# One hybrid network kernel: a ring of PSUM tiles in the first projections, router steps respaced in the dilated attention, second weights and results laid out anew

## The reference

```python
x = x + conv(groupnorm(x)); x = x + spiking_conv(groupnorm(x))   # x [16, 128, 28, 28]
t = tokens(x)                                # [16, 784, 128]
t = t + attention_8_heads(layernorm(t))      # softmax over 784 keys
t = t + top1_of_8_gelu_experts(layernorm(t))
t = t + dilated_attention_16_heads(layernorm(t))   # 256 tokens at rate 1, 512 at rate 2, 16 at rate 4
# last layer: two of 16 experts for each token, xn = layernorm(t)
top_vals, top_idx = top_k(xn @ gate_weight.T, 2); routing_w = softmax(top_vals)
h_mean[e] = sum over the tokens of e of silu(xn @ w1[e].T) / max(count[e], 1)
y_mean[e] = h_mean[e] @ w2[e].T              # [16, 128], zero where count is 0
t = t + sum over the two picks of routing_w * y_mean[top_idx]
```

## Time and profile before

| | |
|---|---|
| time before, median of 3 runs | 3283.76 us (3273.75 to 3286.78) |
| the profiled execution's own time | 3271.72 us |
| its span | 3270.0 us |
| TensorE / VectorE / ScalarE / GpSimd busy | 2786.8 / 2116.2 / 1555.8 / 1036.6 us |
| first projections | 179 to 351 us |
| dilated projections | 1845 to 2056 us |
| dilated attention | 2056 to 2876 us |
| second experts, to the last accumulation | 2903 to 3176 us |
| sums, means, second product | 3176 to 3222 us |
| results | 3222 to 3270 us |

### The profile page before, as it was taken

One profiled execution on the slowest core, in us unless ns is written; L12 is line 12 of the kernel. 1 busy time (PEld: TensorE's weight loads), 2 busy tenths in 40 slices (PEclk: granted clock), 3 DMA queues, 4 the chain that ended last, 5 costly groups with the idle time before them and its releaser, 6 DMA issues. The chain is left out here.

```text
span 3270.0 us, 64262 instructions
## 1 busy us (share of the span) xinstructions
PE 2786.8 (85%) x21148; PEld 1535.5 (47%) x21149; DVE 2116.2 (65%) x3960; ACT 1555.8 (48%) x3276; POOL 1036.6 (32%) x1355
## 2 busy tenths in 40 slices
PE   8978699999999999999399699588888788749998
PEld 4545134433333344333399577355555555413345
DVE  6745677777777777873322266677777777557762
ACT  2235266666666666667155333444544444324440
POOL 0023111222222322222333586245655655620000
PEclk9989699999999999999799899798898888769995
DMA  2024622223222322220322234333333322031132
GB/s 85 1 99 178 135 37 45 42 43 59 42 42 49 51 49 42 43 44 6 99 61 60 65 122 136 98 57 58 61 62 60 62 59 59 24 118 52 53 85 98
DMA packets 208762, 215.87 MB, mean 66 GB/s; under 512 B 32832, under 2 KB 184704, under 8 KB 208512
## 3 DMA queue, kind: packets, MB, share of 16 engines
q1 hardware_dynamic: 180768, 175.54, 23.4%
q0 software_dynamic: 14336, 25.72, 2.9%
q10 hardware_dynamic: 13424, 11.47, 1.2%
HBM read 129.29 MB, written 81.90 MB: 65 GB/s over the span
## 5 line engine op out<-in xcount | busy, mean ns | idle before, releaser
L1586 ACT ACTIVATE attn_exps<-attn_sbank 128x392 f32<-128x392 f32 x1600 | 704.7, 503 | 461.9 <-PE attn_sbank L1503 457.1
L1631 DVE TENSOR_REDUCE attn_mx<-attn_rot 128x1 f32<-128x784 f32 x768 | 722.0, 967 | 185.3 <-PE attn_rot L1516 182.4
L2360 ACT ACTIVATE dil_exps<-dil_sbank 128x512 f32<-128x512 f32 x512 | 289.2, 597 | 360.6 <-PE dil_sbank L2258 357.0
L1516 PE MATMUL attn_rot<-attn_k,attn_q 96*128 96x392 bf16 x1536 | 401.2, 344 | 67.9 <-DVE attn_mx L1631 39.4
L1503 PE MATMUL attn_sbank<-attn_q,attn_k 99*128 99x392 bf16 x1536 | 449.7, 333 | 10.9 <-ACT attn_exps L1586 9.7
L2416 DVE TENSOR_REDUCE dil_mx<-dil_rot 128x4 f32<-128x1024 f32 x256 | 307.3, 1218 | 70.2 <-PE dil_rot L2268 68.0
L1543 PE MATMUL attn_acc<-attn_exps,attn_v 128*32 128x392 f32 x3584 | 348.3, 500 | 0.0
L1503 PEld LDWEIGHTS attn_sbank<-attn_q,attn_k 99*128 99x128 bf16 x1536 | 148.6, 98 | 268.5 <-ACT attn_exps L1586 134.8
L2734 PE MATMUL silu_ph<-silu_route_w,silu_xT 128*128 x424 | 237.6, 645 | 16.7 <-issue 11.9
L1516 PEld LDWEIGHTS attn_rot<-attn_k,attn_q 96*128 96x128 bf16 x1536 | 117.2, 98 | 274.4 <-DVE attn_mx L1631 178.7
L2268 PE MATMUL dil_rot<-dil_k,dil_q 96*128 96x256 bf16 x1024 | 174.1, 299 | 79.7 <-DVE dil_mx L2416 49.1
(11 more groups left out here) (379 smaller groups left out, 4680.2 us busy)
## 6 DMA issues: line engine op xcount, KB each, us to landing
attn_q<-q_pieces SPq DMA_DIRECT2D x192, 98.0 KB, 3.4
attn_k<-k_pieces SPq DMA_DIRECT2D x192, 98.0 KB, 4.6
silu_x<-silu_rows SPq DMA_DIRECT2D x212, 64.0 KB
dil_q<-dil_q_pieces SPq DMA_DIRECT2D x192, 66.0 KB
dil_k<-dil_k_pieces SPq DMA_DIRECT2D x192, 66.0 KB
q_pieces<-qkv_piece SPq DMA_DIRECT2D x16, 588.0 KB, 3.1
k_pieces<-qkv_piece SPq DMA_DIRECT2D x16, 588.0 KB, 3.2
v_rows<-qkv_v SPq DMA_DIRECT2D x16, 476.0 KB, 3.8
```

Of the source, the lines that this page charges most:

```text
L1516: ins = nc.tensor.matmul(rot[b][:, hf, 0:HS], q[nxt.side][g][0:QROWS, j, c * P:(c + 1) * P], k_[nxt.side][g][0:QROWS, j, cols], start=True ...
L1586: nc.scalar.activation(e_[:, n % NP, :], sbank[(n + t.side) % 3][:, 0:HS], ACT.Exp, scale=A_DIM ** -0.5).then_inc(s_ex, 1)
L1631: nc.vector.tensor_reduce(into, rot[b][:, :, 0:HS], AX.XY, ALU.max).then_inc(s_free, 1)
L2360: nc.scalar.activation(e_[:, k % NP, :], sbank[k % 3][:], ACT.Exp, scale=D_DIM ** -0.5).then_inc(s_ex, 1)
```

## The change

It changes three places. The dilated projections, the 8-head attention and the first experts stay as they are.

**The ring, in `attn_inputs`.** The 16 images are written out, without a loop. Four PSUM tiles `pt` are taken in turns by five products of an image: centre and variance, rows, q, k, v. The weights of q, k and v are centred once (`wc`, three matmuls at the start), so that `xn` is `R` times the spread root and `xc` is gone; ScalarE squares the centred tile straight from PSUM. The rows are spread by four matmuls over 64 partitions each. Weights come from ACT's queue, the norm's constants from SP.

**The other end, in `experts_silu` and `finish`.** w2 has SBUF of its own and is loaded in 32 transfers of 128 KB during the tiles. The sums are 16 matmuls of 512 columns with 32 columns of weights, four experts side by side in the array; four copies, two on VectorE and two on ScalarE; 16 matmuls that turn the sums; one scaling into `mean` (in which only every 33rd column is other than zero; it is set to zero at the start); 64 products in four column groups; one product that adds the groups and leaves `ymean` on all 128 partitions. The gates lie at partitions 0, 32, 64 and 96, four images side by side, loaded by four transfers; in `finish` the products of four images use four row groups of the array.

**Dilated attention.** The steps of a turn are placed as in the diff; `rot`'s one semaphore becomes one for each tile; row copies and gate copies go from VectorE to ScalarE; `weigh` is cut into halves of four scores.

```diff
 # attn_inputs: PE's order for an image
+                def rows(n):
                     pe.wait_ge(s_rin, n + 1)
...
+                    for r in (0, 2, 1, 3):
+                        row = slice(64 * (r // 2), 64 * (r // 2) + 64)
+                        at = BANK * (r // 2) + BLK * (r % 2)
+                        ins = nc.tensor.matmul(rows_tile(n)[:, at:at + BLK], spread[row, r, :], rin[row, :], start=True, stop=True)
...
+                    pe.wait_ge(s_xn, n + 1)
+                    if n > 0:
+                        pe.wait_ge(s_rk, n)
+                    product(wc[:, 0, :], xn[j], q_tile(n)).then_inc(s_q, 1)
+                    if n + 1 < B:
+                        variance(n + 1)
+                    if n > 0:
+                        pe.wait_ge(s_vl, n)
+                    product(wc[:, 1, :], xn[j], k_tile(n)).then_inc(s_k, 1)
...
+                    if n + 1 < B:
+                        rows(n + 1)
+                    if n + 2 < B:
+                        pe.wait_ge(s_rq, n + 1)
+                        centre(n + 2)
...
+                    nc.scalar.activation(sq[:], centred_tile(n)[:, 0:S], ACT.Square).then_inc(s_sq, 1)
...
+                    nc.vector.tensor_tensor(halves(xn[n % 2][:]), halves(R[:, n, :]), banks(rows_tile(n)), ALU.mult).then_inc(s_xn, 1)
 # Router: copies on ScalarE
+    def act_rows(self, act, im, rot):
...
+        nc.scalar.activation(self.xc[:, 0:4, :], rot[0:TOK, 0, :].rearrange("k (c d) -> k c d", c=4), ACT.Copy)
...
-            ins = self.nc.vector.tensor_copy(self.turned[:, 4 * TOK * b:4 * TOK * b + cs * TOK], rot[0:self.ex.n, b, 0:cs * TOK])
+            ins = self.nc.scalar.activation(self.turned[:, 4 * TOK * b:4 * TOK * b + cs * TOK], rot[0:self.ex.n, b, 0:cs * TOK], ACT.Copy)
 # dilated_attention: the steps of a turn
+    PICKS_LATE = 10
+    PLACES_AT = {4: (0, 1), 5: (2, 3), 6: (4, 5), 7: (6,), 8: (7, 8), 9: (9, 10)}
+    SCATTERS_AT = {7: 2, 8: 2, 9: 1, 10: 2, 11: 1, 12: 2, 13: 1, 14: 2, 15: 1}
+
+    def late_steps(h, lag):
+
+        out = [("pick", n, lag) for n in range(PICKS_LATE, 16) if (n - PICKS_LATE) // 2 == h]
+        if h == 3:
+            out += [("ranks", lag), ("soft", lag)]
+        out += [("place", n, lag) for n in PLACES_AT.get(h, ())]
+        return out + {10: [("gate", lag)], 11: [("store", lag)]}.get(h, [])
...
-                if (exps and 8 * gr + 10 == n) or (finish and 8 * gr + 10 - D_UN == n):
-                    out.append(("weigh", gr))
-                if (exps and 8 * gr + 13 == n) or (finish and 8 * gr + 13 - D_UN == n):
+                for seg in range(2):
+                    at = 8 * gr + 6 + 4 * seg
+                    if (exps and at == n) or (finish and at - D_UN == n):
+                        out.append(("weigh", gr, seg))
+                if (exps and 8 * gr + 12 == n) or (finish and 8 * gr + 12 - D_UN == n):
...
-                out += {4: [("compact",)], 6: [("den",)], 9: [("add",)], 11: [("rows",)]}.get(h, [])
-                out += [("pick", n) for n in range(16) if 11 + (n + 2) // 4 == h] + [("root",)] * (h == 12)
+                out += {3: [("compact",)], 5: [("den",)], 7: [("add",)], 9: [("rows",)]}.get(h, [])
+                out += [("pick", n, 1) for n in range(PICKS_LATE) if 11 + n // 2 == h]
+                if h == 11:
+                    out.append(("root",))
...
+        def freed(eng, pos):
+            eng.wait_ge(s_free[pos % 2], pos // 2 + 1)
...
-                            if k % 8 == 0:
-
-                                t.wait(act, s_av, lambda e: 4 * e + k // 8 - 1)
+                            if k % 4 == 0:
+
+                                t.wait(act, s_av, lambda e: 8 * e + k // 4 - 3)
 # experts_silu
+                    if t.lo < early_halves:
+                        sp.dma_start(halves[:, t.lo], halves_d[t.lo].rearrange("c f d -> f c d")).then_inc(s_w2, 16)
+                    elif t.lo == UNROLL:
+                        h = t.fours // 2 + early_halves - 1
+                        sp.dma_start(halves[:, bass.ds(h, 1)].rearrange("p o c d -> p (o c) d"), halves_d[bass.ds(h, 1)].rearrange("o c f d -> f (o c) d")).then_inc(s_w2, 16)
...
+                for n in range(4):
+                    for r in range(4):
+                        ins = nc.tensor.matmul(psum_[n][32 * r:32 * r + 32, :], onesc[:], acc[:, 4 * n + r, :], start=True, stop=True)
...
+                        ins = nc.tensor.matmul(px[0][:, E * c + 4 * n:E * c + 4 * n + 4], sums[:, n, c * P:(c + 1) * P], row_pick[:], start=True, stop=True)
...
+                        ins = nc.tensor.matmul(px[1][32 * c:32 * c + 32, 0:P], mean[:, c, 32 * e:32 * e + 32], w2[:, e, c, :], start=(e == 0), stop=(e == E - 1))
...
+                nc.tensor.matmul(ph[0][:, 0:P], comb[:], quarters[:], start=True, stop=True).then_inc(s_y, 1)
...
+                nc.vector.memset(mean[:], 0.0)
 # finish
-                            ins = nc.tensor.matmul(pa[j][:, h, 0:HS], ymean[:], gates_t[:, 4 * i + j, h * HS:(h + 1) * HS], start=True, stop=True)
+                            ins = nc.tensor.matmul(pa[r][:, h, 0:HS], ymean[32 * r:32 * r + E, :], gates_t[32 * r:32 * r + E, i, h * HS:(h + 1) * HS], start=True, stop=True)
```

More of the change, by code:

```diff
@@ L484, in project @@
-                def project(img, i, j, norm_next):
+                for j in two:
+                    ins = nc.gpsimd.memset(v[j][:, 0:FULL, :, A_DIM:], 1.0)
+                ins.then_inc(s_set, 1)
+                for n in range(B):
+                    j = n % 2
                     for t in two:
-                        pool.wait_ge(s_p2, 2 * img + t + 1)
-                        nc.gpsimd.tensor_tensor(piece[j][t][:, 2, :], rest[j][t][:], piece[j][t][:, 1, :],
-                                                ALU.subtract).then_inc(s_p3, 1)
@@ L511, in norm_steps @@
                     ins.then_inc(s_var, 1)
-                    yield
+                def rows(n):
                     pe.wait_ge(s_rin, n + 1)
-                    for r, lo, hi in SPREADS:
-                        ins = nc.tensor.matmul(pr[:, lo:hi], spread[:, r, :], rin[:, lo - r * BLK:hi - r * BLK], start=True, stop=True)
-                    ins.then_inc(s_rb, 1)
-                    yield
-                def norm(n, first):
-                    for _ in norm_steps(n, first):
-                        pass
@@ L580, in _, with square, root @@
-                run(act, norm, project)
+                def square(n):
+                    act.wait_ge(s_c, n + 1)
+                    nc.scalar.activation(sq[:], centred_tile(n)[:, 0:S], ACT.Square).then_inc(s_sq, 1)
+                def root(n):
+                    act.wait_ge(s_var, n + 1)
+                    if n > 0:
+                        act.wait_ge(s_rin, n)
+                    nc.scalar.activation(std[:], var_of(centred_tile(n)), ACT.Sqrt, bias=eps[:]).then_inc(s_std, 1)
+                square(0)
@@ L1996, in dilated_attention, with scatter_steps @@
     GROUPS = 4
-    def route_steps(h, lag):
-        out = []
-        if h == 1:
-            out += [("ranks", lag), ("soft", lag)] + [("place", n, lag) for n in range(5)]
-        if h >= 2:
-            out.append(("scatter", h - 2, lag))
-        if h == 2:
-            out += [("place", n, lag) for n in range(5, 11)]
-        return out + {4: [("gate", lag)], 5: [("store", lag)]}.get(h, [])
+    PICKS_LATE = 10
[7 more added lines that the diff above has]
+        return out + {10: [("gate", lag)], 11: [("store", lag)]}.get(h, [])
+    def scatter_steps(h, lag):
+        before = sum(c for k, c in SCATTERS_AT.items() if k < h)
+        return [("scatter", before + n, lag) for n in range(SCATTERS_AT.get(h, 0))]
     def steps(finish, exps, maxima, older):
@@ L2111, in dilated_attention @@
         s_fill = m.sem("rot_filled")
-        s_free = m.sem("rot_free")
+        s_free = [m.sem(f"rot_free{b}") for b in two]
         s_sc = m.sem("scores_ready")
@@ L2408, in do @@
                     for (x, pos, b, lo) in pipe.turn(t):
+                        im = image_of(t, x)
                         if x[0] == "rows":
                             router.dve_router(dve, prv, rot[b])
-                        if lo is not None:
+                            picks[prv.e], pos_rows[prv.e] = router.dve_picks(dve, prv), pos
+                        if lo is not None and x[0] not in ("rows", "gate"):
                             if x[0] == "turn":
@@ L2677, in experts_silu @@
         ph = [m.ps(f"ph{n}", [P, BANK]) for n in two]
[L2678 to L2679 removed]
+        psum_ = [m.ps(f"psums{n}", [P, BANK]) for n in range(4)]
         s_w = m.sem("weights")
```

562 lines of the change are left out of this document (261 added, 301 removed).

## The result

The median went from 3282.70 us (3273.75 to 3286.78) to 3197.19 us (3195.22 to 3201.68), four runs each: ratio 0.9745, with 95% between 0.9722 and 0.9768. I had said 3137, within 3080 to 3200. The direction held, and the range by 3 us; the gain is 85.5 us where the sum said 147. The two profiled executions are before's shortest (3271.72) and after's longest (3201.68), so that they show 70.1 of it.

What follows compares the result with a forecast made beforehand. TensorE was busy for 85% of the span; in the dilated stage neither it nor VectorE was full, each waiting for the other. Gains 25 + 82 + 21 + 22 − 3 = 147 from 3283.76 gave 3137 us, range 3080 to 3200.

Steps and rivals of the forecast that it cites:

- Part A: Ring in the first projections: 7.8 us an image against 9.41, gain 25 us over 16 images.
- 6.8 + 0.75 = 7.55: First projections, per image: 6.8 us for products that stay, plus 0.75 for the spread if array halves run together.
- my other bound: First projections: gain of 32 us with all edges hidden and the start shortened by a few us.
- Part B: Dilated turn: from 47.8 to 42.5 us, counted 15.5 times, gain 82 us (bounds 10 to 130).
- The floor: Dilated turn: TensorE's 39.15 us busy, below which a turn would not go unless the clock rose.
- the first rival: Dilated turn stays near 45.5 us, two-tile waits, table loads and GpSimd stretching steps; gain 36, total 3183; chance 0.27.
- one of my signs of being wrong: Dilated stage: the forecast would be wrong if a turn stayed over 45 us.
- The copies: Dilated turn: row and gate copies moved to ScalarE take 2.5 us a turn off VectorE.
- the third rival: Dilated turn: ScalarE becomes the ring's bottleneck, 8.1 us a turn against 2.5 saved, turn 53.4, total 3306; chance 0.05.
- Part C's "−3": Set-up and expert tiles: 1.8 us for the memset of `mean`, 1 for late dealt loads; bounds −1 to −12.
- The sums and the results: After the tiles: sums 24.6 us against 45.70, gain 21; results 26 against 48, gain 22.
- The second rival: Projections and results: row groups don't overlap, results gain 0, first projections lose 10 us, total 3169; chance 0.12.

Runs made afterwards that it cites:

- e3: Changed kernel with only the row copies and gate copies put back on VectorE: 3183.29 us (0.9660 to 0.9721 of the kernel before).
- e5: Changed kernel with expert tile loads shared between SP and GpSimd, and the dealt second-weight loads on GpSimd: 3163.01 us.
- e4: Changed kernel with each spread using 128 partitions and the results going through one row group before the next: 3211.47 us.
- e1: Changed kernel with the 32 second-weight loads moved from SP's queue to GpSimd, all issued at the start: 3178.02 us.
- e6: Changed kernel with GpSimd's joining of context parts cut from 512 columns to 16, leaving out most joined contexts: 3148.66 us.
- e7: Changed kernel with the router's square root replaced by a copy, so that its table loads go: 3173.77 us.
- e8: Changed kernel with GpSimd's normalization of the rows moved to the fifth head, away from the picks: 3173.87 us.
- e9: e8 with the second router's root made by Newton steps on VectorE, no table load left: 3172.23 us.

## Why the prediction was right, and where its steps failed

**Part A was right and a little small.** The period is 7.37, below even my 6.8 + 0.75 = 7.55 with all edges hidden, and TensorE has no gap. The rows product at 0.93 lies between the two paces I had bounded it by, 0.75 and 1.4; so it is the products that stay, put at 6.8, that were too dear: 6.4 is left for them. The gain is 32.5, my other bound being 32.

**Part B failed at the 3.4 us that stand on TensorE's 39.15 in the sum of 42.5**, "about 2 us at the rows" and 1.4 before the maximum behind the gate. The floor was right (38.9 busy a turn, clock 0.89). What stands on top was too small and misnamed: 6.9 us of idle time. For the copies of the rows TensorE waits 0.3 a turn (before the gate's product, L1068), for the gate copies not at all. In their place came `ranks` behind held steps (up to 1.9), scores behind the root (1.8) and the split (up to 1.6); the residual's sum (0.9) was there before, and I had no term for it. The turn of 45.7 is the first rival, turn and mechanism, to which I had given 0.27, and one of my signs of being wrong (over 45). I had the stretching in hand and the rule too: the Trainium skill ("SBUF — State Buffer", SBUF: two separate sides) has a VectorE operation with two SBUF inputs and a GpSimd operation that reads SBUF lock one another out of a shared port pair. The rows agree, L942 ending 0.13 us after the L872 that it began beside. I left it out of the forecast because no row told what held L970; the matching timeline of GpSimd, one view more, would have. There, in before, L970 ends 0.13 us after this one:

```profile
2505.71 1.07 POOL L2230 TENSOR_TENSOR dil_o_part<-dil_o,dil_side_of 128x512 f32<-128x512 f32 x1
```

**The copies** stand in the prediction as 2.5 us off VectorE, and in the third rival as 2.5 off the turn itself, though the text says of VectorE and TensorE that "neither is full". Busy time that nobody waits for is not path time, and e3 shows it.

**Part C's "−3" failed, bound and all.** The tiles lost 27.5 and I had allowed 12 at most, by 0.3 for the tile behind each dealt load; it was 1.00. I looked at whether the transfers fit (they do, e5) and at TensorE's 254 us busy, and took the tiles for TensorE's. TensorE's idle time was no sign against it: before, the tiles took 259.7 with 246.14 busy, a gap of 13.6 us, but in e5, where TensorE sets the pace, the gap is 14.9. The sign was that SP hardly ever waited for TensorE (4.1 us), while a busy share doesn't count SP's register and issuing instructions. My own sign of being wrong, that TensorE waits for the dealt weights, came in another form: it waited for the tiles issued behind them.

**The sums and the results** were right in kind and small in size. The sums took 16.1 for my 24.6: L2736 3.6 (I put 6), L2741 3.7 (5), L2747 5.4 (8.6), at a granted clock of 0.89 where the earlier trace rows has 0.66. The results took 24.1 for 26, VectorE back to back as forecast.

**The second rival is out** (e4): 2.1 times faster in four row groups, 1.7 in two. The Trainium skill ("TensorE: Matmul & The Clock Gate", Part 3: Packing small matmuls) has a measured 3.07 times for four; here the products wait for VectorE from the fifth image on, so the rows can't show the full ratio. **The third** is out too: ScalarE is busy for 24.5 of a turn and no turn is over 47.4.

So 147 fell to 70 in the profiles by two sizes, 58 in the turns and 27 in the tiles, then 4 ahead of the tiles and 8 of scatter, with 19 coming back in A, the sums and the results. That the time stayed inside the range, 3 us from its end, owes something to errors of both signs, and so to luck.

Open: why SP's pauses are longer in e1 than before (7 us of the tiles); how e6's 48 us part into held steps, late GpSimd work and TensorE's clock; and which of part B's remaining changes gained its 28 us.

## What to carry to other kernels

Before adding an issue to a queue, look whether that queue ever waits for its consumer: one that hardly ever does was the bound here, however idle the page shows it. When steps of VectorE are spread out, lay GpSimd's timeline beside the new places, since a step of 0.26 us can last as long as the GpSimd instruction that it meets. And a stall taken away is worth its length only until the next one in line: three different cures (e7, e8, e9) stopped near 44. Look at TensorE's busy time and granted clock beside the waits: e7 gained by these alone.

## What the runs showed of the hardware that was not expected

- A tile load whose address comes from a table costs its issuing queue 1.24 us (before), and one further issue in 8 adds 1.00. Over 212 tiles that is 259.7 and 287.2 us; with two queues, where TensorE sets the pace, 257.2.
- A VectorE step of 112x7 elements (L957, 0.166 us) took 0.954 on average in e8: 1.12 in the six of nine turns in which it began behind GpSimd's L2210 of 1.27 us, 0.17 in the two in which it began just before it, and once 1.54. The loss goes by GpSimd's instruction and not by the step's own size.
- TensorE's granted clock fell to its lower level behind waits of 1.5 to 1.9 us in after's turns (0.88 from first to last maximum). In e7 TensorE had 5.6 us more of idle time there and was 25.8 us sooner done, at 0.91.
